# Moving an expert's up and down products between the gaps of a search, in a fused attention and mixture-of-experts kernel

## What is computed

```python
norm = layer_norm(feat, ln_g, ln_b)            # 2048 tokens, 256 wide
scores = norm @ centroids.T                    # 8 experts
# expert after expert takes the 256 best-scored tokens that are still free
for e in range(E):
    s = where(taken, -inf, scores[:, e]); idx = top_k(s, C); taken[idx] = True
h = layer_norm(routed, ln_g, ln_b)             # routed = feat[sort_by_expert]
h = gelu(einsum('ecd,edf->ecf', h, w1) + b1)   # up product, f = 1024
h = einsum('ecf,efd->ecd', h, w2) + b2         # down product
out = routed + h                               # put back in the tokens' order
```

## Time and profile before

| | us |
|---|---|
| median of 3 runs | 313.31 (312.78 to 313.41) |
| the profiled execution | 312.71 |
| its span, first to last instruction | 310.9 |
| granted TensorE clock over the span | 0.994 |

### The profile page before, as it was taken

The page is one execution under the profiler, slowest core; times in us unless marked ns, Lnnn a source line. Parts: engine busy times, 40 slices in busy tenths (PEclk is TensorE's granted clock), DMA queues, the critical chain, the costliest instruction groups (busy, mean ns, idle before and its releaser), DMA issues.

```text
span 310.9 us, 6807 instructions
## 1 busy us (share of the span) xinstructions
PE 292.0 (94%) x2149; PEld 252.9 (81%) x2151; DVE 229.5 (74%) x801; ACT 153.4 (49%) x282; POOL 194.7 (63%) x246
## 2 busy tenths in 40 slices
PE   8999998999999999999997779999999999998990
PEld 3999897999999999999872239898989888888990
DVE  0669999888878888888877877767676767338450
ACT  1357646355555555554554225363636353577720
POOL 8200334467878787787733445768787878859831
PEclk9999999999999999999999999999999999999997
DMA  7995002971000000001101321554656565624110
GB/s 256 353 375 197 3 0 79 382 250 35 36 34 34 34 34 34 34 34 67 38 34 70 136 67 36 174 167 179 198 181 198 190 196 177 209 62 143 53 65 19
DMA packets 21769, 37.79 MB, mean 122 GB/s; under 512 B 2416, under 2 KB 14960, under 8 KB 21360
## 3 DMA queue, kind: packets, MB, share of 16 engines
q1 hardware_dynamic: 19184, 31.16, 28.9%
q0 software_dynamic: 2560, 6.31, 6.6%
HBM read 31.17 MB, written 6.29 MB: 120 GB/s over the span
## 4 chain that ended last, share of the span: by engine, by line
PE 78%; DVE 10%; POOL 5%; issue 3%; ACT 2%; ACTq 0%; POOLq 0%; DVEq 0%
PE pair L1178 68%; PE pair L1254 4%; PE pair L1228 2%; DVE cmpb L994 2%; POOL w1p L508 2%; POOL out_dram L529 2%; PE pair L1266 1%; PE pair L1422 1%; DVE sm L851 1%; DVE wneg L765 1%; DVE pair L1028 1%; POOL G L498 1%; DVE ok L1011 1%; POOL pr L278 0%; POOL yT L514 0%
## 5 line engine op out<-in xcount | busy, mean ns | idle before, releaser
L1178 PE MATMUL pair<-yT,w1p 128*128 128x256 f32 x384 | 54.0, 290 | 0.3 <-POOL yT L514 0.3
L1178 PE MATMUL pair<-Bm,pT 128*128 (+1 forms) x384 | 50.4, 287 | 0.2 <-ACT pT L603 0.2
L1178 PEld LDWEIGHTS pair<-yT,w1p 128*128 128x128 f32 x384 | 48.4, 190 | 1.2 <-POOL yT L514 0.5
L1178 PE MATMUL pair<-Am,xTp 128*128 (+1 forms) x192 | 48.3, 400 | 0.0
L1178 PEld LDWEIGHTS pair<-Bm,pT 128*128 128x128 f32 x384 | 47.1, 191 | 0.4 <-issue 0.4
L1178 PE MATMUL pair<-w2s,hT 128*128 128x256 f32 x192 | 47.1, 389 | 0.0
L278 POOL TENSOR_TENSOR pr<-pr,rs 128x1024 f32<-128x1024 f32 (+1 forms) x16 | 31.3, 1954 | 24.4 <-DVE rs L858 15.3
L508 POOL TENSOR_TENSOR w1p<-w1s,w1p 128x512 fp32r<-128x512 f32 x32 | 40.0, 1273 | 5.4 <-ACT w1p L669 5.3
L1178 PEld LDWEIGHTS pair<-Am,xTp 128*128 128x128 f32 x192 | 34.9, 188 | 7.0
L1178 PEld LDWEIGHTS pair<-w2s,hT 128*128 128x128 f32 x192 | 33.8, 190 | 4.3
L714 ACT ACTIVATE hT<-pair,b1s 128x256 f32<-128x256 f32 x48 | 20.2, 471 | 33.8 <-PE pair L1178 33.8
(11 more groups left out here) (153 smaller groups left out, 573.5 us busy)
## 6 DMA issues: line engine op xcount, KB each, us to landing
w1s<-w_dram SPq DMA_DIRECT2D x8, 1024.0 KB, 5.3
w2s<-w_dram SPq DMA_DIRECT2D x8, 1024.0 KB, 5.9
rows_scratch<-row SPq DMA_DIRECT2D x16, 256.0 KB, 2.0
xs<-x_dram SPq DMA_DIRECT2D x1, 2048.0 KB, 17.2
xTs<-xT_dram SPq DMA_DIRECT2D x1, 2048.0 KB, 18.9
wk_s<-wk_dram SPq DMA_DIRECT2D x1, 1024.0 KB, 5.3
wv_s<-wv_dram SPq DMA_DIRECT2D x1, 1024.0 KB, 7.5
wqT_s<-wqT_dram SPq DMA_DIRECT2D x2, 512.0 KB, 9.0
```

The lines of the kernel that those rows point to most:

```text
L1178: return nc.tensor.matmul(out_, l, r, start=start, stop=stop)
```

## The change

Only the order of TensorE's pieces changes, and with it which gelus ScalarE does before the end of a slot. `SPLIT` goes from 6 to 1: experts 1 to 5 now do four up pieces at the end of a slot (0 and 1 in gap 8, 2 and 3 in gap 9) and four in gaps 0 and 1 of the next, like experts 6 and 7. Their down product begins in gap 2 rather than 3 and ends in gap 7 rather than 8. In the table for these, piece 11 goes from gap 5 to gap 6. Expert 0 stays as it was. No instruction is added or taken away.

```diff
-        SPLIT = E - 2
+        SPLIT = 1
...
             UP_FIRST = {2: {8: (0, 1), 9: (1, 2)}, 4: {8: (0, 2), 9: (2, 4)}}
             UP_REST = {2: {0: (2, 4), 1: (4, 6), 2: (6, 8)}, 4: {0: (4, 6), 1: (6, 8)}}
             DOWN = {2: {3: (0, 3), 4: (3, 6), 5: (6, 8), 6: (8, 10), 7: (10, 13), 8: (13, 16)},
-                    4: {2: (0, 3), 3: (3, 6), 4: (6, 9), 5: (9, 12), 6: (12, 14), 7: (14, 16)}}
-            UP_LATE = {9: (0, 2)}
-
+                    4: {2: (0, 3), 3: (3, 6), 4: (6, 9), 5: (9, 11), 6: (11, 14), 7: (14, 16)}}
             def expert_part(k, gap):
...
                 u = k - 1
                 if 0 <= u < E:
-                    first = UP_LATE if 0 < u < SPLIT else UP_FIRST[first_part(u)]
-                    for f in range(*first.get(gap, (0, 0))):
+                    for f in range(*UP_FIRST[first_part(u)].get(gap, (0, 0))):
                         up(u, f)
```

## The result

The changed kernel takes 315.68 us in the median (315.49 to 316.01, 4 runs) against 313.2 for the kernel before in the same runs: a ratio of 1.0084, with a 95% interval of 1.0071 to 1.0097. By the ratio that is 2.6 us more (2.2 to 3.0), 0.8% slower; the medians differ by 2.5. The forecast was +3.0 us, 316.3.

A forecast was written before the change was run, and what follows sets the result against it. Each gap was bound by the longer of TensorE's work and VectorE's round. Slot 2 +1.5, slots 3 to 6 +1.5, slot 7 -0.05 made +2.95 us: 315.7 profiled, 316.3 us median, range 314.3 to 317.5.

The forecast's parts named there:

- What bounds the slots: Slots 3 to 6: a gap lasts the longer of its TensorE work and VectorE's round, about 1.2 us.
- Sum of a slot: Slots 3 to 6: gaps 6, 7 and 8 change by +0.44, -0.23 and +0.17, together +0.38 us a slot.
- Slot 2: Slot 2 does two more first up pieces of expert 1, with nothing to hide in: +1.5 us.
- Slot 7 gives nothing back: Slot 7 loses two up pieces (1.48 us), but its transpositions wait for the gather: only -0.05 us up to tokens(7).
- Rival 1: Slot 7 and the tail: TensorE carries the tail, so added pieces come off again; 314.8 us, chance 0.17.
- The tail hangs on tokens(7): Tail: no TensorE work between tokens(7) and the last 43 up matmuls; the end moves as tokens(7) does, +2.95 us.
- Rival 3: Behind tokens(7): expert 6's gelu and splits set the tail, so the end comes 1.3 us sooner; 312.0 us, chance 0.06.
- Rival 2: Slots 3 to 6: no floor, TensorE's total work unchanged and everything conserved; 313.3 us, chance 0.05.
- rival 4: Gap 8 of slots 3 to 6: the up product waits for its rows, 0.5 us a slot; 318.2 us, chance 0.07.

The follow-up runs named there:

- The two filling runs: Changed kernel plus eight pairs of unused matmuls in slots 3 to 6: in gaps 2 and 7 1.0085, 316.25 us; in gaps 3 and 6 1.0137, 317.9 us.
- the run with expert 5 alone: Kernel before, with expert 5 alone moved to four first up pieces (two go from slot 7 to the end of slot 6): 1.0047, 314.8 us.
- the early list: Expert 7's token list made earlier in slot 7: in the changed kernel 1.0030, 314.38 us; in the kernel before 0.9985, 312.77 us.
- the last run: Kernel before, with expert 7's list made early and expert 5's last three downs behind expert 6's first four up pieces: 0.9955, 311.94 us.

## Why the prediction was right, step by step

- **What bounds the slots.** Right. Gap 7 fell onto its floor with a wait of 0.45 us, and gap 2 stayed at 1.62. The load's wait there was 0.44, not the 0.2 that I named, because the load's lead is used up first. The two filling runs show the holes directly: a slot with two pairs of 0.22 us there is as long as one without, and 0.45 longer with the pairs in the gaps beside them.
- **Sum of a slot.** +0.38 forecast, +0.32 measured. Gap 6 grew to 1.59, not 1.64. Gap 3 took 1.42 instead of 1.47, where I had put nothing. Gaps 8 and 9 came out 0.05 longer together than I had them. That gap 3 is shorter because the total ahead of it now waits, so that TensorE starts the gap with nothing unfinished, is my guess; no run tests it.
- **Slot 2.** +1.5 forecast, +1.45 measured; the run with expert 5 alone gave 1.44 for the same two pieces in slot 6. The trace's 0.123 us a matmul priced it.
- **Slot 7 gives nothing back.** Right. In the run with expert 5 alone TensorE had 0.19 us less to do up to tokens(7) and took 0.15 us more; the 1.29 us less behind it is the tail's matter. With the three downs left behind tokens(7), 0.38 of 1.48 us came back. In the changed kernel it was +0.14, where I had -0.05: the transposition followed its gather's issue by 3.6 us, not 3.4. Rival 1 falls with it: by it, the run with expert 5 alone would have stayed within 0.1 us of before, and it took 1.5 more.
- **The tail hangs on tokens(7).** Right for both kernels (17.08 and 17.00 us). Bringing tokens(7) forward by 0.6 brought the end forward by as much, and moving TensorE's work behind it did nothing. Where I was wrong is a detail: the hole in TensorE's time was 0.85 us and not over one, and it came at 284, where a pair of up pieces waits for a gelu, and not at 277.
- **Rival 3** (expert 6's splits) was refused with "at most 0.3 us", and for this kernel that holds. But it stands close behind: with the gather out of the way it takes the tail at once. My expectation for the early list in the kernel before failed on exactly that. I gave the next chain 0.7 us of room and forgot that in that kernel TensorE has three more down pieces ahead of expert 6's up pieces.
- **Rival 2** (all conserved) is refuted by the slots' 15.62 us and by the time, **rival 4** (a wait in gap 8) by the rows being ready 0.2 us ahead of the matmul that needs them.
- **The size.** 3.0 us forecast, 2.6 measured, 2.8 by the trace. From 2.95 to 2.8 it is -0.2 in the four slots, -0.05 in slot 2, +0.2 in slot 7 and -0.1 behind it.

## What to carry to other kernels

Where two engines take turns in a loop, an engine's filling work has a price per gap: what goes below the other engine's round is lost, what goes above it is paid. Add the gaps up one by one, and look at the wait ahead of the handshake, not at the busy share, which here was 100% with 0.27 us of waiting in two gaps. And work that is moved away from a point that waits for something else (here a gather) is paid where it arrives and hardly repaid where it left: here 1.45 us was paid, and nothing, or at most 0.4, came back. So find these anchors first; the same places are where a reordering can gain, as the last run shows.

## What the runs showed of the hardware

The time from a gather's issue on GpSimd to the matmul that waited for it was 3.4 to 3.7 us in slot 7 in all these profiles. In one profiled execution (the filled gaps 2 and 7) the first gather of slot 5 was later, and TensorE stood still for 1.19 us at a transposition that waits in no other profile:

```profile
244.29 0.41 PE L1422 MATMUL pair<-cst,G 128*128 128x128 f32 x2 [1.19 <-DMA G<-rows_scratch,idx]
```

Its issue on GpSimd was at 239.24, 5.05 us before. A gather with so little room can be a source of spread between executions, besides being an anchor; this was seen once. All of slots 3 to 6 ran, in these profiles, at a granted clock of 1.00 (2.4 GHz), so none of the differences between them is the clock's.
